# Batch 0's norms and residual moved into the end of attention, and the next stage run batch by batch

## The reference, cut to what matters

```
out  = attention(x_normed) + x_normed            # 16 heads of 16, causal, relu on Q, K, V
o    = (out - mean) / sqrt(var + 1e-8)
x1   = gamma * o + x + ffn(x_normed)             # the first layer's result
y1   = (x1 - mean) / sqrt(var + 1e-5)            # rows for the second layer
qkv  = y1 @ w_qkv ;  logits = y1 @ router_w      # 3 x 256 and 16 columns
xl   = sums of y1 over 32 neighbouring rows      # landmarks, 64 per batch
```

## Time and profile before

| | us |
|---|---|
| median of 3 runs (2262.03 to 2265.37) | 2264.32 |
| the profiled execution | 2262.49 |
| its span | 2260.7 |
| PE busy in the span | 1883.5 (83%) |
| DVE busy | 1530.7 (68%) |
| ACT busy | 1060.3 (47%) |
| POOL busy | 474.3 (21%) |

### The profile page before, as it was taken

The page is one execution under the profiler, slowest core; times in us unless marked ns, Lnnn a source line. Parts: engine busy times, 40 slices in busy tenths (PEclk is TensorE's granted clock), DMA queues, the critical chain, the costliest instruction groups (busy, mean ns, idle before and its releaser), DMA issues. The chain is left out here.

```text
span 2260.7 us, 36975 instructions
## 1 busy us (share of the span) xinstructions
PE 1883.5 (83%) x13023; PEld 1021.3 (45%) x13023; DVE 1530.7 (68%) x3904; ACT 1060.3 (47%) x1989; POOL 474.3 (21%) x532
## 2 busy tenths in 40 slices
PE   0999857999999999999999258888528788999997
PEld 0565512233333333333332035655418555888864
DVE  7985567888888888888884484277305698344456
ACT  3554314566666666666667344355103355332210
POOL 1432220000000000000000000100460587566620
PEclk9999958999999999999999679999659899999999
DMA  3476550030303030304000563100320522555555
GB/s 93 139 242 222 190 152 2 1 136 1 135 2 135 2 135 1 135 2 165 27 11 1 184 218 108 38 1 1 132 98 7 188 97 81 176 185 187 185 202 205
DMA packets 160470, 238.72 MB, mean 106 GB/s; under 512 B 18050, under 2 KB 131586, under 8 KB 158626
## 3 DMA queue, kind: packets, MB, share of 16 engines
q1 hardware_dynamic: 128706, 162.81, 22.1%
q0 software_dynamic: 18912, 60.97, 7.1%
q10 hardware_dynamic: 12672, 12.58, 1.6%
HBM read 116.10 MB, written 119.82 MB: 104 GB/s over the span
## 5 line engine op out<-in xcount | busy, mean ns | idle before, releaser
L968 ACT ACTIVATE c_prob<-c_pst 128x512 f32<-128x512 f32 (+1 forms) x1152 | 599.2, 575 | 370.6 <-PE c_pst L926 232.4
L993 DVE TENSOR_REDUCE c_mx<-c_pf 128x1 f32<-128x512 f32 x768 | 507.6, 684 | 89.4 <-PE c_pf L909 89.4
L909 PE MATMUL c_pf<-c_ka,c_qa 97*128 97x512 bf16 (+3 forms) x1280 | 436.2, 359 | 72.4 <-DVE c_mx L993 34.4
L926 PE MATMUL c_pst<-c_qa,c_ka 100*128 100x512 bf16 (+3 forms) x1280 | 426.7, 351 | 17.4 <-DMA c_qa<-c_mT 13.8
L909 PEld LDWEIGHTS c_pf<-c_ka,c_qa 97*128 97x128 bf16 x1280 | 120.8, 98 | 395.7 <-DVE c_mx L993 216.1
L942 PE MATMUL c_po<-c_prob,c_vh 128*32 128x512 f32 (+3 forms) x2560 | 295.9, 544 | 0.0
L990 DVE CUSTOM_DVE_ANT_0 c_spare<-c_pf,c_cut 128x384 f32<-128x384 f32 (+3 forms) x512 | 243.3, 483 | 42.9 <-PE c_pf L909 41.7
L926 PEld LDWEIGHTS c_pst<-c_qa,c_ka 100*128 100x128 bf16 x1280 | 124.8, 98 | 107.2 <-ACT c_prob L968 23.6
L1765 POOL DMA_INDIRECT s_parts<-x_yr,x_tags x144 | 141.0, 979 | 85.6 <-DVE x_yr L2376 62.3
L884 POOL IOTA c_zero<- 128x24 int32 x6 | 1.3, 211 | 739.3 <-PE c_po L942 739.3
L2263 PE MATMUL x_ps<-x_gu,x_xs 128*128 x576 | 137.7, 383 | 0.0
(11 more groups left out here) (337 smaller groups left out, 2977.9 us busy)
## 6 DMA issues: line engine op xcount, KB each, us to landing
s_slots<-c_zero POOLq DMA_DIRECT2D x6, 3264.0 KB, 22.7
x_xr<-s_slots SPq DMA_DIRECT2D x72, 272.0 KB
x_rows<-s_parts SPq DMA_DIRECT2D x8, 2048.0 KB, 8.4
c_qa<-s_qs SPq DMA_DIRECT2D x32, 384.0 KB
c_ka<-s_ks SPq DMA_DIRECT2D x32, 384.0 KB
s_vs<-b_va SPq DMA_DIRECT2D x32, 256.0 KB, 3.7
c_vh<-s_vs SPq DMA_DIRECT2D x8, 1024.0 KB, 16.8
s_qs<-b_parts SPq DMA_DIRECT2D x16, 384.0 KB, 2.7
```

What stands on the lines that cost most here:

```text
L909: nc.tensor.matmul(pf[:, i % NF, 0:kn], qa[0:R0, s, fh, qt * P:(qt + 1) * P], ka[0:R0, s, fh, k0:k0 + kn], start=True, stop=True).then_inc ...
L926: mm = nc.tensor.matmul(pst[:, u % NS, at:at + qn], ka[0:R1, s, hh, kt * P:(kt + 1) * P], qa[0:R1, s, hh, qb * QB + q0:qb * QB + q0 + qn], ...
L968: nc.scalar.activation(prob[:, g % NP, hh, 0:w], pst[:, u % NS, 0:w], ACT.Exp).then_inc(exp_ok, 1)
L993: nc.vector.tensor_reduce(mx[:, fh, qt, part:part + 1], pf[:, i % NF, 0:kn], AX.X, ALU.max).then_inc(max_ok, 1)
```

## The change

1. `attention`: `c_att` has two buffers instead of eight; each quad's result is stored as soon as it is there, and DVE waits for the store of quad n - 2 before it writes quad n. The zero fills are spread: fill n, then store n.
2. After the store of quad 5 (`n == NQ - 3`) POOL waits for batch 0's stores and then runs `sum_ahead` for each of batch 0's four chunks: seven transfers from POOL's own queue (normed rows, x, ffn, four pieces of the attention result), a wait for all of them, then two additions of 128x1024.
3. DVE gets 44 "slices" (`ahead`): 8 of statistics (two rows of tiles each), one of variance with a first guess of the root by a bit trick, one of three Newton steps and a reciprocal, 8 of normalising, 8 for gamma and residual (one 128x1024 operation each), then 8 + 1 + 1 + 8 for the second norm. They are put in front of every second "score" step behind the last "first", "max" or "rows" step; the first waits for all of POOL's sums. What has found no such place by the end of the list runs behind the last "turn".
4. SP stores batch 0's x1 at the end of attention. x1's sums and y1 stay in SBUF, in the space of `QT`, which is now allocated ahead of attention.
5. `join_and_project`: chunks 0 to 3 are batch 0 and need only turn and products, from the rows kept in SBUF, which SP also stores to `s_rows` at the start. Batch 1's chunks 4 to 7 go through the old chain as m = 0 to 3. Step i of the new order (`in_turn`) has turn(i), products(i - 1), attended(i), normed_attention(i - 1), sum_up(i - 2), second_norm(i - 3) and so on. The weights are loaded first, gamma after the first chunk.
6. `two_layers`: three `cleanup_on_exit` instead of two, the additional one between the first stage and attention.

```diff
+            def sum_ahead(c):
+                tiles = slice(c * TT, (c + 1) * TT)
+                rows = lambda a: a.rearrange("(n p) c -> p n c", p=P)[:, tiles, :]
+                pool.dma_start(ahead_a[:, c], rows(xn_dram)).then_inc(ahead_in, 16)
+                pool.dma_start(ahead_r[:, c], rows(x_dram)).then_inc(ahead_in, 16)
+                wait(pool, sum_ok, 2 * c)
+                pool.dma_start(ff[:], rows(ffn_dram)).then_inc(part_in, 16)
+                for q in range(NQB):
+                    pool.dma_start(part[:, q], att_dram[:, q, tiles, :]).then_inc(part_in, 16)
+                pool.wait_ge(ahead_in, 32 * (c + 1))
+                pool.wait_ge(part_in, 16 * (1 + NQB) * (c + 1))
+                a = ahead_a[:, c].rearrange("p t (q e) -> p q t e", q=NQB)
+                nc.gpsimd.tensor_tensor(a, a, part[:], ALU.add).then_inc(sum_ok, 1)
+                pool.wait_ge(sum_ok, 2 * c + 1)
+                nc.gpsimd.tensor_tensor(ahead_r[:, c], ahead_r[:, c], ff[:], ALU.add).then_inc(sum_ok, 1)
...
             for n in range(NQ):
+                pool.wait_ge(values_ok, (n + 1) * NG)
+                if n < NSLOT // NZ:
+                    fill(n)
                 pool.wait_ge(att_ok, n * NB + NB)
-                pool.dma_start(att_dram[:, n:n + 1], att[:, n:n + 1]).then_inc(att_out, 16)
+                pool.dma_start(att_dram[:, n:n + 1], att[:, n % 2:n % 2 + 1]).then_inc(att_out[n % 2], 16)
+                if n == NQ - 3:
+                    for i in range(2):
+                        pool.wait_ge(att_out[i], 16 * NQB // 2)
+                    for c in range(NCH):
+                        sum_ahead(c)
...
+            LAST = max(j for j, s in enumerate(steps) if s[0] in ("first", "max", "rows"))
+            slices = 0
+            for j, (kind, n, a, hh) in enumerate(steps):
+                if kind == "score" and j > LAST and hh % 2 == 0 and slices < 5 * H + 4:
+                    ahead(slices)
+                    slices += 1
...
+            for i in range(slices, 5 * H + 4):
+                ahead(i)
...
+            def ahead_scale():
+                for _ in range(3):
+                    step_a(nc.vector.reciprocal(root[:], one[:]))
+                    step_a(tt(root[:], var[:], root[:], ALU.mult))
+                    step_a(tt(root[:], root[:], one[:], ALU.add))
+                    step_a(ts(one[:], root[:], 0.5, None, ALU.mult))
+                step_a(nc.vector.reciprocal(scale[:], one[:]))
...
 # join_and_project, SP
+            load_attention(0)
+            sp.dma_start(G[:], gamma.unsqueeze(0).to_broadcast([P, C])).then_inc(w_in, 16)
+            load_rest(0)
+            for n in range(NCH):
+                sp.dma_start(place(rows_dram, n), ahead[:, n]).then_inc(ahead_out, 16)
+            load_attention(1)
+            in_turn([(1, NCH - 1, lambda m: load_rest(m + 1)), (2, NCH - 2, lambda m: load_attention(m + 2)), (1, N, store_turned)])
 # ACT
+            in_turn([(0, N, take), (1, N, take_queries), (1, NCH, normalise(0, o, o, normed)), (2, NCH, root(1)), (0, NCH, root(0)),
+                     (2, NCH, store), (1, N, take_values), (3, NCH, normalise(1, x1, y1, y1_ok)), (4, NCH, store_normed)])
 # PE
-            staggered(pe, N, DEPTH, [(4, turn), (5, products)])
+            in_turn([(0, N, turn), (1, N, products)])
 # DVE
+            in_turn([(1, NCH, normed_attention), (2, NCH, sum_up), (0, NCH, attended), (1, N, pool_rows), (3, NCH, second_norm)])
```

More of the change, by code:

```diff
@@ L786, in attention @@
     rec = sb("c_rec", [P, 4, HQ])
-    att = sb("c_att", [P, NQ, KT, HQ * D])
+    att = sb("c_att", [P, 2, KT, HQ * D])
+    G = sb("c_gamma", [P, C])
+    TT, NCH, NQB = 4, KT // 4, NQ // B
+    part = sb("c_part", [P, NQB, TT, C // NQB])
+    ff = sb("c_ff", [P, TT, C])
+    stats = sb("c_stats", [P, KT, 6])
+    mean, diff, var, root, one, scale = (sb(f"c_{n}", [P, KT]) for n in ("mean", "diff", "var", "root", "one", "scale"))
+    g_in, part_in, ahead_in, sum_ok = sem("c_g_in"), sem("c_part_in"), sem("c_ahead_in"), sem("c_sum_ok")
+    ahead_chain, x1_ok, x1_out = sem("c_ahead_chain"), sem("c_x1_ok"), sem("c_x1_out")
+    A_, R_ = (a.rearrange("p c t e -> p (c t) e") for a in (ahead_a, ahead_r))
     pf = ps("c_pf", [P, NF, W1])
@@ L879, in _, with fill @@
             pool.wait_ge(zero_ok, 1)
-            for g in range(NSLOT // NZ):
-                pool.wait_ge(values_ok, (g + 1) * NG)
+            def fill(g):
                 if g:
@@ L1101, in _, with load_attention, load_rest @@
         def _(sp):
-            sp.dma_start(G[:], gamma.unsqueeze(0).to_broadcast([P, C])).then_inc(w_in, 16)
+            def load_attention(m):
+                s, n = m % 2, NCH + m
+                wait(sp, o_ok, m - 1)
+                sp.dma_start(xn[:, s], place(xn_dram, n)).then_inc(in_ok[s], 16)
+                for q in range(NQ):
+                    sp.dma_start(at[:, s, q], att_dram[:, NQ + q, m * TT:(m + 1) * TT, :]).then_inc(in_ok[s], 16)
+            def load_rest(m):
+                s, n = m % 2, NCH + m
+                wait(sp, x1_ok, m - 1)
+                sp.dma_start(x[:, s], place(x_dram, n)).then_inc(rest_in[s], 16)
+                sp.dma_start(ff[:, s], place(ffn_dram, n)).then_inc(rest_in[s], 16)
@@ L1150, in normalise, with take @@
                 return body
[L1152 removed]
+            def take(n):
                 act.wait_ge(turn_ok, n + 1)
@@ L1275, in coefficients, with attended @@
                 nc.vector.scalar_tensor_tensor(nb[:, i, s], mv[:, i, s, :, 0], -1.0, nq[:, i, s], ALU.mult, ALU.mult).then_inc(scale_ok[i], 1)
[L1277 to L1281, removed]
+            def attended(m):
+                s = m % 2
+                step = steps(0, m, 3)
+                dve.wait_ge(in_ok[s], m // 2 * 80 + 80)
+                wait(dve, x1_ok, m - 1)
                 ins = tt(o[:, s].rearrange("p t (q e) -> p q t e", q=NQ), at[:, s],
@@ L1299, in sum_up @@
-                wait(dve, y1_ok, n - 1)
+                wait(dve, x1_out[s], m // 2 * 16)
+                wait(dve, y1_ok, m - 1)
                 tt(x1[:, s], o[:, s], x[:, s], ALU.add).then_inc(x1_ok, 1)
[L1301 to L1309, removed]
+                dve.wait_ge(x1_ok, m + 1)
@@ L1310, in pool_rows, with second_norm @@
+                statistics(steps(2, m, 3), x1[:, s], 1, s, 1e-5)
+            def second_norm(m):
+                wait(dve, y1_ok, m - 1)
+                coefficients(steps(3, m, 5), 1, m % 2, m)
+            def pool_rows(n):
+                b, u = divmod(n, NCH)
                 dve.wait_ge(xs_ok, n + 1)
                 for k in range(K):
-                    nc.vector.tensor_reduce(xl[:, k, s * M + u * (CH // L):s * M + (u + 1) * (CH // L)],
-                                            xs[:, s, k, :].rearrange("p (l n) -> p l n", n=L), AX.X, ALU.add).then_inc(ls_ok, 1)
```

298 lines of the change are left out of this document (190 added, 108 removed).

## The result

| us | before | after |
|---|---|---|
| median of the compared runs (lowest to highest) | 2264.85 (2262.03 to 2266.09) | 2230.34 (2229.04 to 2236.16) |
| profiled execution, span | 2262.49, 2260.7 | 2231.07, 2229.3 |
| last division of attention | 1259.25 | 1263.05 |
| T0, start of `join_and_project` | 1265.09 | 1275.05 |
| last group of `e_pq` starts (after T0) | 1447.09 (182.0) | 1411.43 (136.4) |

The ratio is 0.9856 [0.9844, 0.9868], a gain of 34.5 us. Forecast were 2223.9 us and a gain of 40.4; the time lies in the range of 2207 to 2246. The two profiled spans differ by 31.4 us, and the stretches of the table split that: T0 is 10.0 later, the stage is 45.6 shorter, and what follows it is 4.3 longer.

A forecast was written before the change was run, and what follows sets the result against it. PE was taken to idle behind the first chunks' norm chain in `join_and_project`, then to set the pace. Terms +5.4 + 1.2 + 1 - 48 = -40.4 us gave 2222.1 profiled, 2223.9 as median; range 2207 to 2246.

The forecast's parts named there:

- attention's body: Attention: POOL's additions holding DVE, plus queueing of small row transfers, taken as +1 us; the additions alone bounded 0 to 15.3.
- last division to T0 (tail and cleanup): End of attention: slices behind the last turn move T0 by +5.4 us, the additional cleanup between stages adds +1.2.
- stage: `join_and_project`: products start about 6 us after T0 instead of 57.7; 134 us instead of 182, a gain of 48 (30 to 64).
- behind the stage: After `join_and_project`: the prediction's sum had no term for this part.
- Rival 1: `join_and_project`: loads come in time, PE bounds from the first products; stage 118 us, kernel 2208; chance 0.13.
- Rival 2: `join_and_project`: ACT's order costs more; stage 152 us, +6 in attention for POOL's lock, kernel 2248; chance 0.17.
- Tail: Behind attention's last turn: 11 slices on the path, together 9.1 us (8 to 11), the 16 normalising at about 0.27 each.
- sign of error: Attention: a body before 1257 grown by more than 5 us was one of the signs that the prediction was wrong.
- POOL's sums: Attention: 21 us a chunk, 85 for four, done about 1160 us, 55 ahead of DVE's first slice; additions 1.91 each.
- Rival 3: Attention: POOL's sums come late, DVE and PE stop; 40 us gain lost from about 45 us a chunk; chance 0.06.

The follow-up runs named there:

- second pair: The profiles of b0 and a0, the kernel before and the changed kernel run again on other chips; medians 2198.61 and 2168.87 us.
- a0: The changed kernel run again without any edit, on another chip; 2168.87 us, ratio 0.9867 to the kernel before.
- e_laahead: Changed kernel with SP issuing the attention loads of batch 1's third and fourth chunk ahead of the x and ffn loads; 2156.18 us, ratio 0.9808.
- e_all: Changed kernel with POOL's additions split, three slices moved earlier, both SP load reorderings, and y1 scaling ahead of V's copy; 2135.77 us, ratio 0.9718.
- b0: The kernel before run again without any edit, on another chip; 2198.61 us, ratio 0.9998.
- e_noadd: Changed kernel with POOL adding 16 elements a partition in place of 1024, loads kept, batch 0's sums left out; 2160.09 us, ratio 0.9827.
- e_split: Changed kernel with each POOL addition made as four instructions of 256 elements a partition; 2160.10 us, ratio 0.9819.

## Why the prediction was right, and where it was off

The mechanism was right where most of the gain lies, in the stage; the smaller term of attention was mis-sized.

| step | forecast | first pair of profiles | second pair |
|---|---|---|---|
| attention's body | +1 (0 to 15.3) | +3.8 | +8.4 |
| last division to T0 (tail and cleanup) | +6.6 | +6.2 | +6.2 |
| stage | -48 (-30 to -64) | -45.6 | -45.1 |
| behind the stage | 0 | +4.3 | -0.4 |
| sum | -40.4 | -31.4 | -30.9 |

The median of the first pair fell by 34.5, 3 us more than its spans. That the forecast misses by 6 us and not by 9 is luck of the executions compared; on the chip of a0 the medians fell by 30.6. The range was 39 us wide, so that the time lies in it says little about the small terms.

- **Stage.** Right in its mechanism and nearly in its size. Products(0) at T0 + 5.6 (forecast 6), its stop 3.25 (3), the stop of products(2) 4.37 (3 to 4), turn(4) at T0 + 65.5 (62.5) behind 9.54 us of idleness (7); from turn(4) on 70.9 (71.5). Of the 2.4 us missed, 3.0 were lost ahead of turn(4) and 0.6 won behind it. That the loop is x1_ok, load, `attended`, root is shown by the rows and by e_laahead: with the load taken out from behind x1_ok, 9.2 us of the stop fall to 1.05.
- **Rival 1** said that only TensorE would bound, at 118. That wasn't so in the changed kernel (136.4), and it is nearly so in e_all (117.1): the size was sound, and the loads and ACT's order were what stood between. Part of that agreement is chance, since e_all still has stops of 2.5 and 3.3 us in products(0) and products(1). **Rival 2** had the right places, ACT's root and copies, and too high a price (152); its +6 for the lock is nearer to what was measured than my +1.
- **Tail.** The slices took 10.4, not 9.1: the sixteen normalising operations 0.33 each in place of 0.27. The cleanup and landing part was then smaller, 1.2 behind the last slice, and the sum of both is right. The extra stage boundary early in the kernel cost nothing that shows: attention starts 1.6 us later (285.64, before 284.06), and by the third division the shift is gone; in the second pair a0 is 0.5 us ahead of b0 there.
- **Attention's body: the step that was mis-sized.** I had +1 as the answer to "what POOL costs DVE", because DVE's bulk there is reductions. But DVE's small operations sit in the chain from the maxima to the next matmuls, and there a held one delays TensorE. "Could wait 1.9 us each", written for the two-input ones, was the measured size (1.9 to 2.2 an operation; casts with one input are held as well), and I gave it no weight in the sum. The clock that TensorE loses by these stops (3.4 us in a0 by the estimate above) was in no term at all. What is held depends on where the additions fall: two operations for 1.8 us or more in after and 3.4 us at the 27th division, three in a0 and 8.9 us lost, 1.8 with instructions of a quarter of the length. e_noadd and e_split show the cause. The prediction's own sign of error, a body longer by more than 5 us, stays out in the first pair (3.8) and comes in the second (8.4). The rule that DVE and GpSimd lock a shared pair of ports (the Trainium skill, SBUF — State Buffer, "Who interferes with whom") is borne out by the held rows, 1.99 and 1.91 us in after.
- **POOL's sums.** An addition took 2.35, not 1.91; a chunk took some 15 us, not 21: its seven issues take 4.4 us in a0, and POOL then waits 4.8 to 6.6 us (after; 21.3 in the first chunk, beside a fill) for the last landing, where I had 17 for both. The last addition ended at 1129, 31 us before my date and 86 before it was needed. Rival 3 was never near.
- **Behind the stage.** 4.3 us on the first chip are in no step of mine. On that chip both kernels have waits in the inverse's iterations for which the profile names nothing on the core as the releaser ("remote"); b0 and a0 have none of them. By the view of waits (us in total, times, longest), after:

```profile
DVE i_X L2078 <- remote: 60.9, 5, 45.8
```

and before:

```profile
DVE i_X L1928 <- remote: 45.4, 2, 34.5
```

The second pair shows no such growth, so nothing ties it to the change. What these waits are stays open; nothing was run on it.

## What to carry to other kernels

Work put on a second engine "beside" a busy one must be priced by what it does to the shortest operations of the critical chain, not to the largest: cut POOL's elementwise instructions short (256 elements a partition here) where DVE's small ones stand on the path. A stop of TensorE can cost more than its length, so look at the granted clock behind it. When a stage is turned from "prepare, then compute" to "chunk by chunk", follow each load back to the wait in front of it in its queue: one load issued behind another operand's buffer wait cost 10 us here, and moving it was a one-line edit. And when a filler hides under idle time up to the last step, count what is left behind that step (10.4 us here) and draw it forward as far as the idle time lasts.

## What the runs showed of the hardware

- A DVE `CAST` of 16 elements a partition with a single input is held as long as a two-input addition when POOL adds two SBUF tiles: 1.99 (after) and 2.21 us (a0) instead of 0.18.
- The held operation ends with POOL's instruction (in after at 1111.63 and 1114.06, POOL's at 1111.60 and 1114.03). Four POOL instructions of 256 elements take 2.78 us in place of 2.35, and the longest held operation in attention is then 0.69 (e_split).
- Behind such stops TensorE's granted clock fell from 1.00 to 0.85 and 0.83 over 20 us (a0), and stayed at 1.00 in the same stretches where the additions were short or left out (e_split, e_noadd). In a0 TensorE waited 1.49, 1.59 and 2.72 us for `c_mx` inside them or up to 4 us ahead of them.
- POOL's addition of 128x1024 f32 took 2.35 us during attention; of the same shape, L2023 took 1.91.
- The same kernel differs by 66 us between chips (2264.85 and 2198.6), of which most lies behind the projecting stage (813.6 and 749.9).
